# Mixture-of-experts stage: first and third products on the two row halves of TensorE's array at once, three passes each, and down products in batches of four tiles

## The reference, cut to what matters

```
flat = _rmsnorm(x, ln2_w).reshape(-1, Cx)                # 2048 x 64
probs = jax.nn.softmax(flat @ router_w.T, axis=-1)       # 8 experts
tp, ti = jax.lax.top_k(probs, TOPK)
...
for e in range(NE):                                      # 8 experts, hidden size 170
    hh = jax.nn.silu(flat @ w1[e].T) * (flat @ w3[e].T)
    out = out + weights[:, e:e + 1] * (hh @ w2[e].T)
```

## Time and profile before

| | us |
|---|---|
| median of 3 runs (262.27 to 262.62) | 262.43 |
| the profiled execution, device time | 261.8 |
| its span in the profile | 260.1 |
| TensorE matmul busy | 225.7 (87%) |
| VectorE busy | 181.6 (70%) |
| ScalarE busy | 163.3 (63%) |
| GpSimd busy | 148.2 (57%) |

### The profile page before, as it was taken

The page is one execution under the profiler, slowest core; times in us unless marked ns, Lnnn a source line. Parts: engine busy times, 40 slices in busy tenths (PEclk is TensorE's granted clock), DMA queues, the critical chain, the costliest instruction groups (busy, mean ns, idle before and its releaser), DMA issues.

```text
span 260.1 us, 6594 instructions
## 1 busy us (share of the span) xinstructions
PE 225.7 (87%) x2456; PEld 156.2 (60%) x2465; DVE 181.6 (70%) x428; ACT 163.3 (63%) x293; POOL 148.2 (57%) x189
## 2 busy tenths in 40 slices
PE   8978879879998999997688788997689898999986
PEld 3645446447685786885566566763346465566665
DVE  4137557942478578678998977956988669986582
ACT  2478763769877597763455436565667966666660
POOL 6997001113377575374083678568887576677780
PEclk9999999999999999999999999999999999999999
DMA  2576100000000000000000000000000000000010
GB/s 42 142 179 145 39 4 1 3 0 0 3 1 3 0 0 4 3 1 0 3 0 3 0 3 1 3 3 0 0 5 4 0 3 20 3 13 10 3 25 20
DMA packets 7467, 4.48 MB, mean 17 GB/s; under 512 B 6500, under 2 KB 6796, under 8 KB 7436
## 3 DMA queue, kind: packets, MB, share of 16 engines
q1 hardware_dynamic: 7436, 4.06, 6.7%
HBM read 3.53 MB, written 0.52 MB: 16 GB/s over the span
## 4 chain that ended last, share of the span: by engine, by line
PE 50%; DVE 27%; ACT 9%; issue 9%; POOL 3%; DVEq 0%; ACTq 0%; POOLq 0%
PE bank L1242 48%; DVE nmx L1032 3%; DVE shared L1205 3%; ACT shared L719 1%; ACT qT L607 1%; DVE early L779 1%; DVE shared L890 1%; ACT early L498 1%; PE bank L1460 1%; POOL shared L406 1%; DVE s L882 1%; DVE oT L1059 1%; ACT shared L587 1%; DVE ex L1040 1%; ACT qT L732 1%
## 5 line engine op out<-in xcount | busy, mean ns | idle before, releaser
L1242 PE MATMUL bank<-early 64*64 64x256 f32 (+4 forms) x561 | 58.2, 352 | 11.6 <-DVE early L779 2.7
L406 POOL TENSOR_TENSOR shared<-shared 128x512 f16<-128x512 f32 x44 | 51.0, 1159 | 18.4 <-ACT shared L719 17.0
L1242 PEld LDWEIGHTS bank<-early 64*64 64x64 f32 (+3 forms) x561 | 31.3, 126 | 30.3 <-issue 5.4
L1205 DVE SCALAR_TENSOR_TENSOR shared<-bank,qT 128x512 f32<-128x512 f32 x44 | 30.1, 688 | 13.7 <-ACT qT L732 12.3
L344 POOL TENSOR_TENSOR stat<-stat,neghalf 128x4 f32<-128x4 f32 x16 | 16.2, 1012 | 37.6 <-DVE stat L864 28.2
L732 ACT ACTIVATE qT<-bank 128x512 f32<-128x512 f32 x44 | 26.2, 597 | 13.7 <-PE bank L1242 13.6
L1242 PE MATMUL bank<-qT,shared 128*128 128x256 f32 x112 | 31.2, 388 | 3.9 <-DVE shared L890 3.1
L719 ACT CAST shared<-shared 128x512 f16<-128x512 f32 x44 | 27.0, 614 | 7.8 <-DVE shared L1205 7.3
L1242 PE MATMUL bank<-onehot,w3h 128*128 128x512 f16 x88 | 26.3, 380 | 3.7 <-DVE shared L1205 3.4
L439 POOL TENSOR_TENSOR oTx<-oT,oTx 128x512 f16<-128x512 f32 x16 | 19.0, 1188 | 18.0 <-ACT oTx L619 18.0
L1242 PE MATMUL bank<-onehot,w1h 128*128 128x512 f16 x88 | 26.2, 379 | 0.0
(11 more groups left out here) (225 smaller groups left out, 490.2 us busy)
## 6 DMA issues: line engine op xcount, KB each, us to landing
early<-in_tcn_w_dram SPq DMA_DIRECT2D x2, 320.0 KB, 4.4
w1s<-in_w1m_dram SPq DMA_DIRECT2D x2, 256.0 KB, 3.7
qT<-in_w3m_dram SPq DMA_DIRECT2D x2, 256.0 KB, 3.5
out_dram<-L SPq DMA_DIRECT2D x8, 64.0 KB, 1.9
qw<-in_attn_q_dram SPq DMA_DIRECT2D x2, 128.0 KB, 2.9
hTs<-in_w2m_dram SPq DMA_DIRECT2D x1, 256.0 KB
cos<-in_cos_t_dram SPq DMA_DIRECT2D x2, 96.0 KB, 2.3
sin<-in_sin_t_dram SPq DMA_DIRECT2D x2, 96.0 KB, 2.6
```

Of the source, the lines that this page charges most:

```text
L406: nc.gpsimd.tensor_tensor(hhx[:, i, 1, :], hh[:, u % RING, :], hhx[:, i, 0, :], ALU.subtract).then_inc(S["lo_ready"], 1)
L1205: V_.scalar_tensor_tensor(hh[:, u % RING, :], bank[2 + u % 2][:, :], HH_SCALE / FFN_SCALE, sil[:, u % 2, :], ALU.mult, ALU.mult).then_inc( ...
L1242: return nc.tensor.matmul(out_, l_, r_, start=a, stop=z, skip_group_check=skip)
```

## The change

The token rows are laid out anew: the high part stands in both partition halves, and so does the low part, as two arrays of 512 columns (`fT2[p]`, `x_ = 0` high, `x_ = 1` low). The first product reads partitions 0 to 63 of rows and weights, the third reads 64 to 127; they are issued in turn, three passes each: high by high, high by low, low by high. The product of the two low parts is left out; the router keeps all four. The down products of a `k` are issued for all four tiles together, after chunks 1, 3, 6 and 9, and the first `sum_up` moves from chunk 2 to chunk 3, `mix` of `k = 2` from chunk 1 to chunk 2. For the new layout ScalarE copies both parts once more (`f_twice`), the transposes of a block are 8 in place of 4, `f_rows` copies a whole bank in place of half of one, and the router does 16 matmuls of 64 rows in place of 8 of 128.

```diff
-        fTs = onehot[:, :, :].rearrange("p a b -> p (a b)").bitcast(f16).rearrange("p (g c) -> p g c", c=P)
+        fT2a = onehot[:, :, :].rearrange("p a b -> p (a b)").bitcast(f16).rearrange("p (a x t) -> p a x t", a=2, x=2)
+        fT2b = sTs[:, :, :].rearrange("p g t -> p (g t)").rearrange("p (a x t) -> p a x t", a=2, x=2)
+        fT2 = [fT2a[:, 0], fT2a[:, 1], fT2b[:, 0], fT2b[:, 1]]
...
+            def f_twice(p):                                    # ScalarE
+                act.wait_ge(S["fsplit_ready"], p + 1)
+                nc.scalar.copy(shl[:, p % 2, :, 0:4:3, :], shl[:, p % 2, :, 1:3, :]) \
+                    .then_inc(S["f_twice"], 1)
             def f_rows(p, b_):
                 act.wait_ge(S["trf_ps"], p + 1)
-                nc.scalar.copy(fTs[:, 4 * p:4 * p + 4, :].rearrange("p a b -> p (a b)"),
-                               bank[b_][:, 0:256].bitcast(f16)).then_inc(S["fTs_ready"], 1)
+                nc.scalar.copy(fT2[p].rearrange("p x t -> p (x t)"), bank[b_][:, :].bitcast(f16)) \
+                    .then_inc(S["fTs_ready"], 1)
...
+                if b in (5, 6):
+                    f_twice(b - 5)
...
             for u in range(PAIRS * CH):
+                if u == 1:
+                    f_twice(2)
                 if u == 4:
                     f_rows(2, 6)
+                if u == 8:
+                    f_twice(3)
...
-                if n_ and i == 1:                              # VectorE
+                if n_ and i == 2:
                     mix(n_ - 1, 2, 4)
...
             def f_transposed(p, b_):                           # TensorE
-                pe.wait_ge(S["fsplit_ready"], p + 1)
+                pe.wait_ge(S["f_twice"], p + 1)
...
-                for a in range(4):
-                    r = nc.tensor.transpose(bank[b_][:, 64 * a:64 * a + 64].bitcast(f16),
-                                            shl[:, p % 2, a, 1:3, :].rearrange("p a b -> p (a b)"), ident16[:, :])
+                for x_ in range(2):
+                    for a in range(4):
+                        r = nc.tensor.transpose(bank[b_][:, 256 * x_ + 64 * a:256 * x_ + 64 * a + 64].bitcast(f16),
+                                                shl[:, p % 2, a, 2 * x_:2 * x_ + 2, :].rearrange("p a b -> p (a b)"),
+                                                ident16[:, :])
...
-                    for w in range(2):
-                        r = mm(bank[b_][:, c_ + NE * a:c_ + NE * a + NE], fTs[:, 4 * p + a, :], rwh[:, w, :], w == 0,
-                               w == 1)
+                    for i, (x_, w) in enumerate(((0, 0), (0, 1), (1, 0), (1, 1))):
+                        r = mm(bank[b_][:, c_ + NE * a:c_ + NE * a + NE], fT2[p][0:64, x_, P * a:P * a + P],
+                               rwh[0:64, w, :], i == 0, i == 3)
...
-                for w_, b0, read, done in ((w1h, 0, "sil_ready", "a_ps"), (w3h, 2, "hh_ready", "b_ps")):
...
-                    for w in range(2):
-                        r = mm(bank[b0 + u % 2][:, :], w_[:, w, ORDER[i], :], rhs, w == 0, w == 1)
-                    r.then_inc(S[done], 1)
+                for k_, (x_, w) in enumerate(((0, 0), (0, 1), (1, 0))):
+                    for w_, half, b0, read, done in ((w1h, lo_, 0, "sil_ready", "a_ps"),
+                                                     (w3h, hi_, 2, "hh_ready", "b_ps")):
+                        if k_ == 0:
...
+                            if u >= 2:
+                                pe.wait_ge(S[read], u - 1)
+                        r = mm(bank[b0 + u % 2][:, :], w_[half, w, ORDER[i], :], fT2[n_][half, x_, :], k_ == 0, k_ == 2)
+                        if k_ == 2:
+                            r.then_inc(S[done], 1)
...
-                if n_ and i == 0:
-                    down(n_ - 1, 2, 2)
-                    down(n_ - 1, 2, 3)
-                if n_ and i == 2:
-                    down(n_ - 1, 3, 0)
-                    down(n_ - 1, 3, 1)
+                if n_ and i == 1:
+                    for t_ in range(4):
+                        down(n_ - 1, 2, t_)
+                if n_ and i == 3:
+                    for t_ in range(4):
+                        down(n_ - 1, 3, t_)
                     sum_up(n_ - 1, 0)
-                if n_ and i == 3:
-                    down(n_ - 1, 3, 2)
-                    down(n_ - 1, 3, 3)
-                if i == 5:
-                    down(n_, 0, 0)
-                    down(n_, 0, 1)
                 if i == 6:
-                    down(n_, 0, 2)
-                    down(n_, 0, 3)
+                    for t_ in range(4):
+                        down(n_, 0, t_)
                     if n_:
                         sum_up(n_ - 1, 2)
-                if i == 8:
-                    down(n_, 1, 0)
-                    down(n_, 1, 1)
                 if i == 9:
-                    down(n_, 1, 2)
-                    down(n_, 1, 3)
-                if i == 10:
+                    for t_ in range(4):
+                        down(n_, 1, t_)
+                if u == PAIRS * CH - 1:
                     down(n_, 2, 0)
                     down(n_, 2, 1)
```

More of the change, by code:

```diff
@@ L181, in tower @@
                  "sum_ps", "added", "fin_ready", "wts_ready", "w1cast", "w2_scaled", "w2_cast", "hx_ready", "hi_ready", "lo_ready",
-                 "wt_zero_low", "wt_zero_high"]
+                 "wt_zero_low", "wt_zero_high", "f_twice"]
         S = {n: sem(n) for n in names}
@@ L197, in tower @@
         GATE_STEPS = ((1, 2, 3), (8, 9, 13), (19, 20, 22), (24, 25, 27))
-        ROUTE_BANK = ((1, 0), (1, 0), (6, 256), (6, 288))
+        ROUTE_BANK = ((1, 0), (1, 0), (6, 0), (6, 0))
         geP = bank[7][:, 0:256].rearrange("p (a i j) -> p a i j", a=4, j=NE)
@@ L1746, in _ @@
                 n_, i = u // CH, u % CH
-                rhs = fTs[:, 4 * n_:4 * n_ + 4, :].rearrange("p a b -> p (a b)")
                 if i == 0:
                     pe.wait_ge(S["fTs_ready"], n_ + 1)
-                for w_, b0, read, done in ((w1h, 0, "sil_ready", "a_ps"), (w3h, 2, "hh_ready", "b_ps")):
[L1751 to L1758, removed]
-                    for w in range(2):
-                        r = mm(bank[b0 + u % 2][:, :], w_[:, w, ORDER[i], :], rhs, w == 0, w == 1)
-                    r.then_inc(S[done], 1)
+                if u == 0:
+                    pe.wait_ge(S["wlow_ready"], 2)
+                for k_, (x_, w) in enumerate(((0, 0), (0, 1), (1, 0))):
+                    for w_, half, b0, read, done in ((w1h, lo_, 0, "sil_ready", "a_ps"),
+                                                     (w3h, hi_, 2, "hh_ready", "b_ps")):
+                        if k_ == 0:
+                            if u == 0:
+                                pe.wait_ge(S["nmT_ready" if b0 == 0 else "ym_ready"], B if b0 == 0 else TILES)
+                            if u == 1:
+                                pe.wait_ge(S["rexp_in" if b0 == 0 else "max_ready"], 2 if b0 == 0 else 3 * B)
+                            if u >= 2:
[3 more added lines that the diff above has]
+                            r.then_inc(S[done], 1)
                 if u == 3:
```

## The result

The changed kernel takes **268.69 us** (median of 4 runs, 268.27 to 269.69) against 262.47 for the kernel before, measured beside it: a ratio of 1.0243, 95% interval 1.022 to 1.0266. That is slower by 6.2 us, inside the range of 264.5 to 271.5. The profiled execution took 268.36, with a span of 266.7 against 260.1.

What follows compares the result with a forecast made beforehand. TensorE was taken to bound the last block, a chain over VectorE much of the rest. Terms 3.2 + 1.2 + 0.2 + 1.1 = 5.7 over 261.8 gave 267.5, forecast as a median of 268.1 us, range 264.5 to 271.5.

Steps and rivals of the forecast that it cites:

- Pairs at 0.216, a unit of 0.65, changes of 0.1: TensorE's expert units: row halves overlap fully, three 0.216 us steps a unit; each change between half and full rows costs 0.1.
- The wait of the third unit, 0.91: Where three units stand in a row, the third waits 0.91 us for its bank; three such waits a block, 2.7.
- Last block +1.2: Last of the mixture's four blocks: 18.1 us in place of 16.9, plus 1.2.
- Tail +0.2: At the end, the last silu comes 0.2 us later in its unit.
- Attention stage +1.1: Batch rows 6 and 7: more transposes and small matmuls on TensorE, 0.55 us counted for each row, plus 1.1.
- Blocks 0 to 2, +3.2: First three mixture blocks: delays put the start of the last block 3.2 us later; range 1.5 to 5.
- Silu 14: Checkpoint after block 0's late table load: silu of unit 14 predicted at 206.5, plus 1.8 us.
- it is now VectorE's chain, of unchanged length, up to the product of unit 28: After product 19, plus 2.0 us: VectorE's chain adds no further delay, putting unit 28's product at 231.6, not 229.53.
- TensorE's busy time down: Expected sign in the changed kernel's timeline: TensorE busy for less time, VectorE's busy time the same; no size given.
- Rival A: Faster: third-unit wait not 0.91 us; without it the last block gains 1.6, whole 260.9; chance 0.16.
- Rival B: A wash: idle time takes in delays of blocks 0 to 2, attention stage hides its work; 262.3 us, chance 0.06.
- rival C: Row halves don't run together: six passes, 1.30 us a unit, whole about 285; chance 0.07, partial overlap included.

Runs made afterwards that it cites:

- experiment 5: Changed kernel with the third product read from the same row half as the first, so they can't run together: 283.08 us in the profiled run, against 262.73.
- experiment 4: Changed kernel with a third bank for the third product in the last block only: 266.56 us, ratio 1.0174 to the kernel before.
- experiment 3: Changed kernel's row layout alone, with the old full-row passes and old places of the down products: 264.23 us, ratio 1.0069 to the kernel before.
- experiment 2: Kernel before with only the down products batched for all four tiles, full-row passes kept: 262.01 us against 262.56, ratio 0.9982.
- experiment 1: Changed kernel with the down products handed out two tiles at a time, as before the change: 266.55 us, ratio 1.0152 to the kernel before.
- experiment 6: Changed kernel with a third bank for the third product in all blocks and the gates' scratch moved to SBUF: 273.92 us, ratio 1.0433 to the kernel before.
- experiment 9: Kernel before with batched down products and the gates' scratch moved from bank 7 to SBUF, full-row passes, two banks: 271.77 us, ratio 1.0356.
- experiment 8: Kernel before with batched down products, plus pairs and a third bank in the last block only: 262.45 us against 262.62, ratio 0.9997.
- experiment 7: Kernel before with batched down products, third bank in all units and gates' scratch in SBUF, full-row passes: 269.9 us, ratio 1.026, clock partly down.

## Why the prediction was right

The forecast was 268.1 and the median 268.69; slower, by the mechanism named. Step by step:

- **Pairs at 0.216, a unit of 0.65, changes of 0.1:** 0.216 and 0.66 measured. From 249.00, the last pair's start, to the batch at 249.31 is 0.31, 0.1 more than a step. Experiment 5 shows the full overlap that float32 quarters had let me infer. By the ratio of the Trainium skill ("TensorE: Matmul & The Clock Gate", Part 3) for four row tiles it would have been 0.28, an estimate; two halves show no such loss.
- **The wait of the third unit, 0.91:** 0.93 measured, in three groups of the last block; experiment 4 takes it away and gets back 2.2 of the 2.7, the rest being 0.2 at each for silu.
- **Last block +1.2:** +1.29. **Tail +0.2:** +0.27. **Attention stage +1.1:** +1.1 in this profile; experiment 3's 1.4 holds some 0.35 of clock. The eight transposes took 0.61 as worked out, the copy of a whole bank 1.01 for 1.1. The 16 router products took 0.55, 0.21 more than eight did, for my 0.24; the two changes beside them lie outside that row and were not measured.
- **Blocks 0 to 2, +3.2:** +3.57, the term that was mis-sized, by 0.4. Silu 14 came at 208.02 in place of 204.74; less the 1.48 of unit 0, that is 1.8 late, as predicted. Product 19 was 3.42 late, less 1.48, 1.9 for my 2.0. Then the step that failed: "it is now VectorE's chain, of unchanged length, up to the product of unit 28". That product came at 233.47 in place of 229.53, 3.94 less 1.48 or 2.5 late, so that 0.5 was added on the way. The chain shows why: from 221.08 on it is product, TensorE for 3.09, product, TensorE for 4.69. The batches and three-unit waits of block 2 already bound there, while I let them begin at unit 29.
- **+0.4 at the start** was in no term, and I can't tie it to the change.
- **One sign that did not come:** "TensorE's busy time down". It went from 225.7 to 227.5, and in the last block from 16.90 to 17.07. The count takes in each matmul's 0.38 and so most of the short waits; that TensorE has less to do shows in experiment 4's 16.01, not in this number.

As a sum over runs: the layout alone costs 1.7 (experiment 3), the batches alone nothing or less (experiment 2). Pairs with split down products come out 2.3 above the layout (experiment 1), of which the blocks show 1.4 (0.4, 0.8, 0.1 in blocks 1, 2 and last); some 0.9 lies ahead of unit 0, where the two kernels do the same work, and is again of the start. The batches on top cost 2.1 (changed kernel against experiment 1); in the blocks it is 2.7 (0.1, 0.9, 0.5 and 1.2), since experiment 1's unit 0 came 0.8 later. A pair saves 0.22 a unit and pays it in changes, waits for GpSimd and VectorE, or a third-unit wait, whichever is there. What is still open in part is block 1, 20.5 against 19.2 with the layout alone: how much of the 1.3 is waits of third units. The timelines put 0.9 of it ahead of silu 14, which stands 10.49 behind unit 10 in the changed kernel (208.02, 197.53) and 9.60 behind it with the layout alone (207.03, 197.43); there the prediction had the whole down batch ahead of unit 13 and the table load. The other 0.4 comes behind silu 14. No run there took one wait away by itself; the third bank in that block needs the scratch moved, and experiments 6 and 9 show what that costs.

Rival A needed a third-unit wait under 0.5. Experiment 4 makes it 0.2, and the last block does fall to 16.01, 0.9 under the old: about the 1.6 of rival A less three times 0.2. But experiment 8 shows that even then the layout takes the gain back. Rival B, that the other engines' idle time would take in the delays of blocks 0 to 2, falls with the 3.57 lost there, and rival C with experiment 5.

## What to carry to other kernels

Before two products are put side by side, ask what used to run during the second: here silu ran beside the third product, and with the pair both results come late and together. A unit that gets shorter by 0.22 needs one more buffer, or the reader's latency (2.2 us over two banks) becomes the period. Count also what the new layout costs (1.7 here) and each change of shape (0.1), against 2.4 of TensorE a block.

## What the runs showed of the hardware

- Pairs of 64-row float16 matmuls of 512 columns step at 0.216, the same as one full-row one, their starts 0.01 apart; a change between half and full rows costs 0.1.
- Where a GpSimd instruction was running, VectorE's two-input step on SBUF operands took 1.26 in place of 0.43, and a copy within SBUF 0.62 to 0.91 in place of 0.18 (experiment 9). With the scratch in a PSUM bank the same steps take 0.43 and 0.18, beside GpSimd too (kernel before, 183.84 and 183.16).
- The granted clock of experiment 7's profile was at half (0.50) from about 186.5 to 193.4, 203.8 to 207.0 and 234.3 to 237.6, and full between; TensorE had waited 1.79 us up to 186.94, 2.86 up to 202.06 and 2.15 up to 233.65. That makes the 0.83 of two longer stretches, in which TensorE was busy for 24.67 of 30 and 7.84 of 10 us; it was 1.00 from 210 to 230, with 18.76 of 20. The changed kernel, busy 13.48 of 17.30 in block 0, kept the full clock. At half clock a pair stepped by 0.42 (experiment 6, 191.19 to 191.61) in place of 0.216.
